# Layer norm in one pass per tile, and feed-forward products read from PSUM by VectorE, in an attention block with top-k selection

## The reference

```
dots = q k^T * scale                       # 512 x 528, memory keys first
dots = mix over heads by pre_proj; causal mask
vk   = 64th largest of each row; smaller ones are dropped
attn = softmax(dots); mix over heads by post_proj; out = attn v, then @ Wo + bo
```

## Time and profile before

| | |
|---|---|
| median of three executions | 3607.39 us |
| profiled execution, its own time | 3610.26 us |
| its span | 3608.5 us |
| ACT busy | 3177.0 us, 88% |
| DVE busy | 2962.0 us, 82% |
| PE busy | 2833.9 us, 79% |
| POOL busy | 2009.9 us, 56% |
| mean granted PE clock | 0.881 of full |
| transfers | 22.65 MB, mean 6 GB/s |

### The profile page before, as it was taken

How to read it: one execution, slowest core, us unless ns; L and a number is a source line. 1 busy time by engine, 2 the same in 40 slices (tenths; PEclk the granted TensorE clock), 3 DMA queues, 4 the chain that set the end, 5 groups by cost and what they waited for, 6 DMA issues and landing times. The chain is left out here.

```text
span 3608.5 us, 70619 instructions
## 1 busy us (share of the span) xinstructions
PE 2833.9 (79%) x13751; PEld 1830.1 (51%) x13751; DVE 2962.0 (82%) x12236; ACT 3177.0 (88%) x9018; POOL 2009.9 (56%) x3687
## 2 busy tenths in 40 slices
PE   7788787878868887788878768877787888777765
PEld 3455555555545555555555545555455555555544
DVE  4588888888888888888888888888888888888883
ACT  1799999999979999999999979998899999999982
POOL 3355655555555565655655545564655555565544
PEclk9888989898988988888998988988898898989876
DMA  1000000000000000000000000000000000000000
GB/s 41 7 2 2 5 8 5 8 2 5 8 4 8 5 2 8 5 8 5 8 2 5 8 4 8 5 8 2 5 8 5 8 5 2 8 5 8 2 7 4
DMA packets 31403, 22.65 MB, mean 6 GB/s; under 512 B 3201, under 2 KB 30338, under 8 KB 30722
## 3 DMA queue, kind: packets, MB, share of 16 engines
q1 hardware_dynamic: 30722, 16.03, 1.6%
HBM read 11.83 MB, written 4.19 MB: 4 GB/s over the span
## 5 line engine op out<-in xcount | busy, mean ns | idle before, releaser
L881 ACT ACTIVATE signs<-scores,state 128x528 int8<-128x528 f32 (+3 forms) x3072 | 1760.0, 573 | 199.5 <-DVE state L1102 106.6
L1276 POOL TENSOR_SCALAR probs<-probs,rinv 128x528 f32<-128x528 f32 (+3 forms) x1024 | 541.4, 549 | 1416.3 <-DVE rinv L1132 1415.3
L747 PE MATMUL t_bank<-ident,probs 128*128 128x128 f32 x2560 | 519.4, 329 | 590.1 <-POOL probs L1276 540.8
L1284 POOL TENSOR_TENSOR work<-scores,work 128x528 f32<-128x528 f32 (+3 forms) x1024 | 887.6, 903 | 15.8 <-DVE work L1024 15.8
L723 PE MATMUL s_bank<-xn,gT 128*128 128x512 f32 (+3 forms) x2048 | 800.0, 515 | 9.5 <-ACT gT L813 6.8
L734 PEld LDWEIGHTS y_bank<-u_all,probsT 128*128 128x128 f32 x5120 | 631.3, 197 | 135.5 <-issue 122.6
L747 PEld LDWEIGHTS t_bank<-ident,probs 128*128 128x128 f32 x2560 | 312.0, 160 | 712.3 <-issue 554.9
L734 PE MATMUL y_bank<-u_all,probsT 128*128 128x128 f32 x5120 | 636.9, 281 | 7.8 <-ACT probsT L892 7.7
L1127 DVE SCALAR_TENSOR_TENSOR probs<-scores,kth,expo 128x528 f32<-128x528 f32 (+3 forms) x1024 | 521.9, 564 | 82.4 <-issue 70.9
L881 ACT ACTIVATION_READ_ACCUMULATOR signs<-scores,state 128x1 f32 x3072 | 573.8, 187 | 0.0
L1024 DVE TENSOR_SCALAR_CACHE_REDUCE work<-scores,state 128x528 f32<-128x528 f32 (+3 forms) x1024 | 527.6, 553 | 46.6 <-DVE state L1102 41.4
(11 more groups left out here) (148 smaller groups left out, 3240.2 us busy)
## 6 DMA issues: line engine op xcount, KB each, us to landing
xwork<-in_L_attn_x_dram SPq DMA_DIRECT2D x17, 256.0 KB, 2.9
xres<-in_L_attn_x_dram SPq DMA_DIRECT2D x16, 256.0 KB, 3.0
out_dram<-ybuf SPq DMA_DIRECT2D x16, 256.0 KB, 2.4
u_all<-in_L_attn_Wq_dram SPq DMA_DIRECT2D x1, 512.0 KB, 3.8
u_all<-in_L_attn_Wk_dram SPq DMA_DIRECT2D x1, 512.0 KB, 4.6
u_all<-in_L_attn_Wv_dram SPq DMA_DIRECT2D x1, 512.0 KB, 5.4
u_all<-in_L_attn_Wo_dram SPq DMA_DIRECT2D x1, 512.0 KB
expo<-in_L_ffn_w_gate_dram SPq DMA_DIRECT2D x1, 192.0 KB, 4.8
```

The costliest lines, as they stand in the source:

```text
L747: mm = nc.tensor.transpose(t_bank[q % 2][:, at:at + P], probs[:, h % 2, KEY_AT[t] + j * P:KEY_AT[t] + (j + 1) * P], ident[:, :])
L881: nc.scalar.activation(signs[:, k, 0:ROW[t]], row(scores, ring(head_of(s, k + 1), RING), t), ACT.Sign, bias=guesses(s % STATES, k, GUESSES ...
L1276: nc.gpsimd.tensor_scalar(prb, prb, rinv[:, slot_p, t:t + 1], 1.0, ALU.mult, ALU.mult).then_inc(scaled, 1)
L1284: nc.gpsimd.tensor_tensor(wrk, row(scores, slot_k, t), wrk, ALU.subtract).then_inc(hidden, 1)
```

## The change

Layer norm: `norm` replaces the two instructions over 128 x 512 (L1196, L1200) by four over 128 x 128, each subtracting the mean and multiplying by the scale at once; `ln_out` is raised by each, and those who waited for it wait for four. Feed-forward: ACT makes only the tanh of GATE c and nothing for UP c. DVE, at step 10 + c and ahead of the chain that moves the guesses, computes (1 + tanh) times the gate from its PSUM bank, waits for its own result and for UP c, and multiplies by the UP bank. POOL's multiplication is gone. `misc_free` becomes one semaphore per bank, since two engines now free banks. DOWN 0 waits for the bank of UP 2.

```diff
-                            act.wait_ge(silu_ready, HC * (b - 1) + 1)
                             act.wait_ge(misc_full, misc_index(kind, b, use) + 1)
-                            nc.scalar.activation(f_tanh[...], misc[...][:, :], ACT.Tanh, scale=0.5)
-                            nc.scalar.copy(f_gate[:, use[1], :], misc[...][:, :]).then_inc(misc_free, 1)
+                            nc.scalar.activation(f_tanh[...], misc[...][:, :], ACT.Tanh,
+                                                 scale=0.5).then_inc(tanh_ready, 1)
                         elif use[0] == "UP":
-                            take(kind, b, par, use, f_up[:, use[1], :])
+                            pass
...
-                    if 11 <= s < 11 + HC and kind != "first":
-                        c = s - 11
-                        dve.wait_ge(silu_pool, HC * (b - 1) + c + 1)
+                    if 10 <= s < 10 + HC and kind != "first":
+                        c = s - 10
+                        gate_at, up_at = misc_place(kind, par, ("GATE", c)), misc_place(kind, par, ("UP", c))
+                        dve.wait_ge(tanh_ready, HC * (b - 1) + c + 1)
+                        alone(dve)
                         v.scalar_tensor_tensor(out=f_up[:, c, :], in0=f_tanh[:, c, :], scalar=1.0,
-                                               in1=f_up[:, c, :], op0=ALU.add, op1=ALU.mult).then_inc(silu_ready, 1)
+                                               in1=misc[gate_at][:, :], op0=ALU.add, op1=ALU.mult
+                                               ).then_inc(misc_free[gate_at], 1)
+                        dve.wait_ge(misc_free[gate_at], turns_of_bank(kind, b, misc_at(kind, ("GATE", c))) + 1)
+                        dve.wait_ge(misc_full, misc_index(kind, b, ("UP", c)) + 1)
+                        alone(dve)
+                        v.tensor_tensor(f_up[:, c, :], f_up[:, c, :], misc[up_at][:, :], ALU.mult).then_inc(misc_free[up_at], 1)
...
-                nc.gpsimd.tensor_tensor(dst[:, :, :], src[:, :, :], meanvar[:, :, 0:1].to_broadcast([P, T, D]),
-                                        ALU.subtract).then_inc(ln_centred, 1)
-                pool.wait_ge(ln_centred, n + 1)
-                alone(pool)
-                nc.gpsimd.tensor_tensor(dst[:, :, :], dst[:, :, :], rstd[:, :].unsqueeze(2).to_broadcast([P, T, D]),
-                                        ALU.mult).then_inc(ln_out, 1)
+                for t in range(T):
+                    nc.gpsimd.tensor_scalar(dst[:, t, :], src[:, t, :], meanvar[:, t, 0:1], rstd[:, t:t + 1], ALU.subtract,
+                                            ALU.mult).then_inc(ln_out, 1)
...
-                    if 10 <= s < 10 + HC:
-                        c = s - 10
-                        pool.wait_ge(misc_free, misc_index(kind, b, ("UP", c)) + 1)
-                        alone(pool)
-                        nc.gpsimd.tensor_tensor(f_up[:, c, :], f_up[:, c, :], f_gate[:, c, :], ALU.mult).then_inc(silu_pool, 1)
...
 share (PE):
-                at_least(pe, misc_free, misc_index(kind, b, use) - 1)
+                n = misc_at(kind, use)
+                at_least(pe, misc_free[n % 2], turns_of_bank(kind, b, n))
```

More of the change, by code:

```diff
@@ L191, with misc_first @@
 PLACE = {k: {u: i for i, u in enumerate(USES[k])} for k in KINDS}
-def misc_index(kind, b, use):
+MISC_BATCH = len(USES["mid"])
+assert MISC_BATCH % 2 == 0
+def misc_first(kind):
     n = 0 if kind == "pro" else len(USES["pro"])
@@ L413, in build @@
         misc_full = sem("misc_full")
-        misc_free = sem("misc_free")
+        misc_free = [sem(f"misc_free{i}") for i in range(2)]
+        tanh_ready = sem("tanh_ready")
         scores_full = sem("scores_full")
@@ L446, in build @@
         ln_rstd = sem("ln_rstd")
-        ln_centred = sem("ln_centred")
         ln_out = sem("ln_out")
@@ L466, in keys, with freed @@
             return tensor[:, bass.ds(slot, 1), KEY_AT[t]:KEY_AT[t] + KEYS[t]].squeeze(1)
+        def freed(engine, kind, b, n):
+            engine.wait_ge(misc_free[n % 2], turns_of_bank(kind, b, n) + 1)
         def mem_parts(flat):
@@ L706, in memory_y @@
             def memory_y(kind, b):
-                pe.wait_ge(misc_free, misc_index(kind, b, ("PM", 1)) + 1)
+                for i in range(2):
+                    freed(pe, kind, b, misc_at(kind, ("PM", i)))
                 for t in range(T):
@@ L717, in score @@
             def score(kind, b, par, s, g):
-                pe.wait_ge(misc_free, g_index(kind, b, s) + 1)
+                freed(pe, kind, b, g_at(kind, s))
                 for t in SCORE_ORDER:
@@ L812, in take @@
                 act.wait_ge(misc_full, misc_index(kind, b, use) + 1)
-                nc.scalar.copy(dst, misc[misc_place(kind, par, use)][:, :] if src is None else src).then_inc(misc_free, 1)
+                nc.scalar.copy(dst, misc[misc_place(kind, par, use)][:, :] if src is None else src).then_inc(
+                    misc_free[misc_place(kind, par, use)], 1)
             def take_values(kind, b, par, u):
@@ L857, in take_extra @@
                         elif use[0] == "GATE":
-                            act.wait_ge(silu_ready, HC * (b - 1) + 1)
                             act.wait_ge(misc_full, misc_index(kind, b, use) + 1)
-                            nc.scalar.activation(f_tanh[:, use[1], :], misc[misc_place(kind, par, use)][:, :], ACT.Tanh, scale=0.5)
-                            nc.scalar.copy(f_gate[:, use[1], :], misc[misc_place(kind, par, use)][:, :]).then_inc(misc_free, 1)
+                            nc.scalar.activation(f_tanh[:, use[1], :], misc[misc_place(kind, par, use)][:, :], ACT.Tanh,
+                                                 scale=0.5).then_inc(tanh_ready, 1)
                         elif use[0] == "UP":
-                            take(kind, b, par, use, f_up[:, use[1], :])
+                            pass
                         else:
@@ L981, in memory_maxima @@
             def memory_maxima(kind, b, par):
-                dve.wait_ge(misc_free, misc_index(kind, b, ("MEM", 1)) + 1)
+                for half in range(2):
+                    freed(dve, kind, b, misc_at(kind, ("MEM", half)))
                 at_least(dve, masked, 4 * H * b)
@@ L1033, in step @@
                             if p == 2:
-                                dve.wait_ge(misc_free, flag_index(kind, b, s) + 1)
+                                freed(dve, kind, b, flag_at(kind, s))
                                 alone(dve)
@@ L1160, in step @@
                     if s == 15 and kind != "first":
-                        dve.wait_ge(misc_free, misc_index(kind, b, ("DOWN", 1)) + 1)
+                        for i in range(2):
+                            freed(dve, kind, b, misc_at(kind, ("DOWN", i)))
                         norm_stats(kind, b, "Z", ybuf)
@@ L1227, in _ @@
             pool.wait_ge(table_in, 16)
-            pool.wait_ge(misc_free, misc_index("pro", 0, ("NORM",)) + 1)
+            freed(pool, "pro", 0, misc_at("pro", ("NORM",)))
             alone(pool)
```

52 lines of the change are left out of this document (26 added, 26 removed).

## The result

The changed kernel took 3632.65 us in the median of four executions (3625.78 to 3637.16), beside 3607.06 for the kernel before (3604.89 to 3607.62): ratio 1.0070, 95% interval 1.0053 to 1.0088. It is slower by 25.6 us. The forecast was slower by 44, the range 3594 to 3705.

What follows compares the result with a forecast made beforehand. ACT, busy 88%, was taken to set the pace, meeting DVE's guess chain once a step. Terms 97 - 21 + 11 + 9 - 8 - 41 - 3 (drain) gave +44 us: 3651 us, range 3594 to 3705.

Steps and rivals of the forecast that it cites:

- ACT sets the pace and meets DVE once a step at the guesses: ACT's own list sets most steps; its count(2) waits for DVE's chain moving the guesses, 72 times, 106.6 us in all.
- A = end of UP c + 2.6 us: Steps 10 to 12: A, the next count(2)'s start, follows UP c by hand-over, 0.65 product, 1.84 chain and 0.03 to ACT.
- S + 2.64: Mean end of PE's UP c, counted from S, the start of ACT's tanh; the 45 pairs lay between 1.55 and 4.36.
- +97 and +9: Feed-forward steps: A 2.16 us later, 45 times, +97; turn 2, GATE and UP later by 0.3, 30 times, +9.
- The copies of UP c, -21, with +11 back: ACT's copies behind A go, 0.47 each, 45 times, -21; ACT then waits 0.25 each for PE's turn 0, +11.
- The wait for FLAG: FLAG waits for DVE's second product, which ends some 4 us before its turn; costed at nothing.
- Step 13, -8: DVE's product and POOL's 1.27 us before it go, shortening ACT's wait: 0.5 us each, 15 times, -8.
- Norm, -41: POOL's norm 0.78 us shorter, so guesses come sooner in steps 0, 2, 8 and 9: 2.7 us in 15 batches.
- the signs that the prediction named: ACT's guess wait about 176, DVE's UP wait some 60, norm instructions 0.35 to 0.39 each, ACT's busy time down 43 us.
- the norm wins: Rival, 13%: DVE freed of POOL's long instructions, ACT's guess waits in steps 0, 2, 8 and 9 vanish: 3593 us.
- PE at its upper clock: Rival, 10%: UP c ends at S + 1.56, S being the tanh's start, 49 us fewer: 3602 us, no change.
- The last rival: Rival, 2%: DVE finds UP c ready, so 97 + 11 + 9 fall away and a hidden second product stays: 3534 us.

Runs made afterwards that it cites:

- the products behind: The changed kernel with DVE's two products moved behind the chain that moves the guesses, the second behind the reciprocal of the row sums: 3510.56 us, ratio 0.9737.

## Why the prediction came out as it did

The direction and the mechanism came out as forecast, and the size within the range. Laid out as in the prediction's sum, the profiled execution has +78 - 2 - 12 - 48 = +16 us in the 15 batches, where +97 + 9 - 21 + 11 - 8 - 41 = +47 was forecast. That the total came within 19 us of the median is in part luck, since the terms below were off in both directions.

- *ACT sets the pace and meets DVE once a step at the guesses*: right. It is what the feed-forward experiments turned on.
- *DVE waits for UP c, and A = end of UP c + 2.6 us*: right, 2.58. The mean end of UP c was mis-sized: forecast S + 2.64 and later still in the second and third step, measured S + 1.56, 2.88 and 2.30, mean 2.25. The term was +97 and +9; A moved on average from S + 3.10 to S + 4.83, so it is 45 x 1.73 = +78. I had argued that longer waits of PE before turn 0 would bring more of the 1.2 GHz level. In step 10 it was the reverse: UP 0 ended at S + 1.56 in 14 of 15 batches, the value of the quick pair in the earlier trace rows, and it did so with the norm edit alone as well. I had taken UP's time from the trace before, as if the norm edit left it alone. The mean granted clock hardly moved, 0.881 to 0.875.
- *The copies of UP c, -21, with +11 back*: the loss was larger. From A to the end of `count(0)` steps 10 and 12 took 10.04 and 10.05 us before and 9.98 and 10.01 after: about 0.05 gained of 0.47, so the two terms are -2 and not -10. With the products behind it took 9.56, the full 0.47. Against that kernel ACT's copy of turn 0 starts 0.21 and 0.25 us later after `count(1)`, and the copy of the flags another 0.13 later. The wait for FLAG I had costed at nothing; which of PE's or DVE's instructions delays it was not followed.
- *Step 13, -8*: measured -0.79 x 15 = -12.
- *Norm, -41*: alone -35 in the medians and -42 in the 15 batches of the profile, -48 there within the whole change; right in sum and wrong in its working, so the match is luck: two errors went against each other. I priced POOL's instruction at 0.36 to 0.39 us from the scaling of 128 x 144; it took 0.79, because it subtracts. That made the norm 1.0 us longer instead of 0.8 shorter. The gain came all the same, because this form hardly holds DVE (0.1 us, once for each of POOL's instructions), where I had it held in short pieces: step 8 and 9 gave 1.03 and 1.52, step 0 1.03. The price appeared in step 2, where I had forecast a gain of 0.8 and it lost 0.39. Rows of PE and POOL there, PE waiting for XT with `weigh` and `turn` behind it, and ACT's wait a little later:

```profile
1804.96 3.68 POOL L1225 TENSOR_SCALAR xwork<-xwork,meanvar,rstd 128x128 f32<-128x128 f32 x4 [0.18 <-POOL rstd L1221]
...
1808.69 0.69 PE L621 MATMUL misc<-ident,xwork 128*128 128x128 f32 x2 [4.25 <-POOL xwork L1225]
```

```profile
1814.32 0.59 ACT L912 COPY probsT<-t_bank 128x512 f32<-128x512 f32 x1 [2.03 <-PE t_bank L766]
```

The rule of the Trainium skill used in the prediction (SBUF — State Buffer, Who interferes with whom) is that a GpSimd instruction that reads SBUF contends with DVE's two-input ones. It fits the old form and the copy, and not this one: 40 of them ran beside the `tensor_scalar` at 0.27 us or less. The measurement decides.

Of the signs that the prediction named, DVE's wait for UP (44.8 us, forecast 60) and ACT's for the guesses (132.3, forecast 176, with 96 against 118 of it in steps 10 to 12) came, smaller; the length of POOL's four did not. ACT's busy time fell by 32 us instead of 43; with the products behind it fell by 48.

The rival "the norm wins" had the mechanism of the norm nearer than the forecast did: ACT's waits for guesses did fall by two thirds when the norm was changed alone, but more than half of the 68 us turned into the wait for turn 0, and the feed-forward part weighed twice as much. "PE at its upper clock" held in step 10 alone. The last rival, with UP c ready in time, was priced wrong: it took both products as hidden, at 3534. With UP made first (above) it took 3589, since the tanh and two products alone put A at S + 4.04, 0.9 behind the S + 3.10 of before.

## What to carry to other kernels

Ask of a moved or added instruction first what it waits for and what stands behind it in its engine's list: two products of 0.69 us, 45 times each, made the kernel 122 us longer in front of a chain that another engine waits for than behind it, 43 of that by the wait for one input. An instruction removed from the busiest engine is worth its length only where that engine doesn't at once meet the next wait (0.05 of 0.47 us here, all of it once the products were moved). And an operation's price comes from the same arithmetic, not only the same shape: a row with two multiplications priced a subtraction at half.

## What the runs showed of the hardware

On GpSimd, `tensor_scalar` over 128 x 128 fp32 took 0.375 us with multiplications by one scalar per partition and a constant, 0.45 with two scalars per partition and multiplications or an addition, 0.72 and 0.79 with a subtraction, in first or in second place, and 0.60 for a subtraction alone. DVE instructions with two SBUF inputs, 0.16 us by themselves, took up to 1.08 us beside a GpSimd `tensor_tensor` over 128 x 512 of 1.04 us, 0.58 beside a copy over 128 x 512 of 0.63, and mostly 0.16, at times 0.26 and at most 0.34 beside `tensor_scalar` over 128 x 128 with scalars per partition. DVE's products with one operand in PSUM took 687 and 688 ns, as with both in SBUF (695, rows 3).
